# Sixteen indirect stores of a routing list, held one by one for the exponentials of the next batch's causal attention

## The reference

```python
att = jnp.einsum('bhqd,bhkd->bhqk', q, k) / jnp.sqrt(jnp.float32(hd))
att = jnp.where(causal, att, -jnp.inf)
att = jax.nn.softmax(att, axis=-1)
y = jnp.einsum('bhqk,bhkd->bhqd', att, v)
...
logits = flat @ gate_W + gate_b
top_v, top_i = jax.lax.top_k(logits, TOP_K)
w = jax.nn.softmax(top_v, axis=-1)
w_full = w_full.at[jnp.arange(N)[:, None], top_i].add(w)
for e in range(NUM_EXPERTS):
    mid = jax.nn.gelu(flat @ exp_W1[e] + exp_b1[e], approximate=False)
    out = out + w_full[:, e:e + 1] * (mid @ exp_W2[e] + exp_b2[e])
```

## Time and profile before

| | us |
|---|---|
| median of 3 runs (lowest, highest) | 4084.98 (4074.66, 4093.1) |
| the profiled execution | 4093.66 |
| its span, first to last instruction | 4091.9 |
| TensorE busy in it (matmuls) | 3443.6 |
| VectorE busy | 2301.5 |
| ScalarE busy | 1529.2 |
| GpSimd busy | 432.3 |

### The profile page before, as it was taken

The page is one execution under the profiler, slowest core; times in us unless marked ns, Lnnn a source line. Parts: engine busy times, 40 slices in busy tenths (PEclk is TensorE's granted clock), DMA queues, the critical chain, the costliest instruction groups (busy, mean ns, idle before and its releaser), DMA issues.

```text
span 4091.9 us, 55117 instructions
## 1 busy us (share of the span) xinstructions
PE 3443.6 (84%) x21294; PEld 1851.1 (45%) x21294; DVE 2301.5 (56%) x5198; ACT 1529.2 (37%) x2358; POOL 432.3 (11%) x323
## 2 busy tenths in 40 slices
PE   7788887787797589998889888898888988889988
PEld 5333333433432378886445324463244543344532
DVE  7664663673664356665643565634657246564356
ACT  5354343434334234443542323523234332254232
POOL 0000000001001134443000020000210001100002
PEclk9899898989989789999999998998998999999989
DMA  7401400410320497775111302113021032201130
GB/s 280 108 10 64 116 10 7 161 22 5 133 53 2 77 264 222 222 228 154 25 27 27 69 6 58 27 25 66 5 53 34 4 38 58 50 15 27 27 69 11
DMA packets 197242, 292.19 MB, mean 71 GB/s; under 512 B 88125, under 2 KB 154319, under 8 KB 180241
## 3 DMA queue, kind: packets, MB, share of 16 engines
q1 hardware_dynamic: 179957, 268.10, 24.8%
q0 software_dynamic: 17024, 20.53, 2.5%
HBM read 210.02 MB, written 77.23 MB: 70 GB/s over the span
## 4 chain that ended last, share of the span: by engine, by line
PE 55%; DVE 24%; ACT 8%; DMA 6%; issue 5%; SPq 1%; POOL 1%; another core or an unknown queue 0%; DVEq 0%; ACTq 0%; POOLq 0%
PE ps L877 6%; DVE max_parts L2097 5%; PE ps L827 5%; PE ps L829 4%; PE ps L828 4%; PE ps L1036 4%; PE ps L1265 3%; PE ps L1272 3%; PE ps L996 3%; PE ps L1158 2%; PE ps L1419 2%; PE ps L1019 2%; DMA q_stack<-in_exp_W 2%; PE ps L1193 2%; ACT arena L1538 2%
## 5 line engine op out<-in xcount | busy, mean ns | idle before, releaser
L877 PE MATMUL ps<-ternary_W,ident 128*128 128x512 f16 x2260 | 677.2, 415 | 134.4 <-ACT arena L1665 40.8
L2097 DVE TENSOR_REDUCE max_parts<-ps 128x1 f32<-128x512 f32 (+3 forms) x768 | 384.4, 551 | 196.4 <-PE ps L999 122.4
L1538 ACT ACTIVATE arena<-ps 128x256 f32<-128x256 f32 (+7 forms) x512 | 318.8, 650 | 447.3 <-PE ps L1019 258.0
L877 PEld LDWEIGHTS ps<-ternary_W,ident 128*128 128x128 f16 x2260 | 226.9, 105 | 454.4 <-issue 152.5
L1848 POOL TENSOR_TENSOR arena<-arena 128x640 f32<-128x640 f32 x96 | 154.9, 1614 | 1999.8 <-ACT arena L1770 1998.6
L2017 DVE CAST arena<-arena 128x256 f16<-128x256 f32 (+2 forms) x424 | 162.0, 382 | 255.0 <-ACT arena L1702 136.0
L1604 ACT ACTIVATE arena<-ps 77x1024 f32<-77x1024 f32 x192 | 190.6, 1017 | 196.7 <-PE ps L1185 194.0
L1770 ACT ACTIVATE arena<-ps 128x1024 f32<-128x1024 f32 x128 | 130.7, 1024 | 335.2 <-PE ps L1408 328.9
L996 PE MATMUL ps<-k_stack,q_stack 96*128 96x512 f16 (+3 forms) x576 | 196.6, 378 | 65.5 <-DVE max_parts L2097 32.8
L2019 DVE TENSOR_TENSOR arena<-arena 128x256 f16<-128x256 f32 (+2 forms) x424 | 241.6, 570 | 14.7
L2532 DVE TENSOR_REDUCE max_parts<-ps 128x1 f32<-128x512 f32 x256 | 166.5, 686 | 143.1 <-PE ps L1392 141.3
(11 more groups left out here) (444 smaller groups left out, 7395.4 us busy)
## 6 DMA issues: line engine op xcount, KB each, us to landing
arena<-scr_expert_weights SPq DMA_DIRECT2D x52, 1024.0 KB
k_stack<-scr_expert_weights SPq DMA_DIRECT2D x26, 1024.0 KB
q_stack<-in_exp_W SPq DMA_DIRECT2D x16, 1024.0 KB
scr_expert_weights<-k_stack SPq DMA_DIRECT2D x16, 1024.0 KB, 4.9
q_stack<-scr_q SPq DMA_DIRECT2D x108, 128.0 KB, 3.8
scr_q<-arena SPq DMA_DIRECT2D x48, 256.0 KB, 2.3
k_stack<-scr_q SPq DMA_DIRECT2D x72, 128.0 KB, 4.7
scr_q<-arena SPq DMA_DIRECT2D x16, 512.0 KB, 4.2
```

Source lines behind the costliest of these rows:

```text
L877: pe.matmul(s[:, 0:CH], ident[:], Wq1[:, 0, 0:CH], start=True, stop=True)
L1538: act.activation(PR[:, n % NP, kt * P:T], slot(L, "ST", g, kt, j)[:, kt * P:T], ACT.Exp).then_inc(*did("act", L, "exp", g, kt, j))
L2097: dve.tensor_reduce(mpart[:, j * NT + t, c:c + 1], slot(L, "S", g, t, j, c)[:, 0:n], AX, ALU.max).then_inc(*frees("dve", L, "S", g, t, j, c))
```

## The change

The first of a batch's sixteen stores goes out as before, when the list's entries are there. Each of the other fifteen first waits for one exponential of the next batch's attention: that of the last head (j = 3) of the tiles (2, 0), (2, 1) to (3, 6) in turn, the two last groups of heads. The stores themselves, their order and what they write are the same. For the last batch, which has no batch after it, nothing changes.

```diff
--- before.py
+++ after.py
@@ -1794,8 +1794,12 @@
             def note_places(b):
 
                 pool.wait_ge(*of("dve", "RT", "entry", batch=b))
+                among = [(g, kt) for g in range(2, NG) for kt in range(NT)] if b + 1 < NB else []
                 for t in range(NT):
                     for i in range(2):
+                        if among and t + i:
+                            g, kt = among[2 * t + i - 1]
+                            pool.wait_ge(*of("act", "B0", "exp", g, kt, GH - 1, batch=b + 1))
                         pool.indirect_dma_start(d_tab, bass.IndirectOffsetOnAxis(ap=slots_now[:, t, i:i + 1], axis=0),
                                                 entry[:, t, i], None).then_inc(*did("st_tab", b, t, i))
```

## The result

The changed kernel takes 4048.0 us, the median of five runs (4043.68 to 4052.79). The kernel before, timed again beside it, takes 4086.42 (five runs, 4074.66 to 4093.1). The ratio is 0.990, its 95% interval 0.9883 to 0.9916: 38.4 us saved, between 34 and 48 us by the interval. The forecast was 4043 with 42 us saved.

A forecast was written before the change was run, and what follows sets the result against it. It took sixteen crowded stores delaying TensorE's signals in three batches' attention as the loss on the path that sets the end. 42.85 us regained less 1 for moved stores, 42 rounded, off the 4084.98 median gave 4043 us; range 4030 to 4076.

The forecast's parts named there:

- The size of the loss: Attention from the tick (once-per-group reduction) of g = 2 to that of g = 3: batches 1 to 3 lose 42.85 us against batch 0.
- The cost of a spread store: Each of 45 moved stores was priced at 0.02 us, 1 us in all; bounds were zero and 0.89 us each.
- Stage A: Attention from the tick (once-per-group reduction) of g = 2 to that of g = 3; forecast at 43 to 46 us in all batches.
- Who is late: Beside the row of stores, TensorE's signals to ScalarE and VectorE come late, by 7.2 us, though their inputs are ready.
- something was still empty: Feared error: the row's first stores were free only because something was empty that a later isolated store finds full; no size.
- Crowding: The forecast's case: only a row of stores at 1.27 us delays TensorE's signals; 4043 us, chance 0.79.
- The ports rule: Skill page on SBUF ports: DMAs and compute cannot slow each other, so the saving would be zero instead of 42 us.
- not the stores: Rival: the attention loss stems from the routing itself, the stores only lie beside it; no change, 4085 us, chance 0.04.
- The sum: Whole kernel: 42.85 us regained less 1 us for the moved stores, rounded to 42 us gained.
- all later stages shift earlier with it: Stages after the shortened attention stage hang on signals, so the 42 us saved reaches the end.
- rival on the slower side: Each moved store in the attention catches a TensorE signal: 95 us lost against 43 gained, +52, 4137 us; chance 0.07.
- stage g = 3: From the tick of g = 3 to the end of the attention's exponentials; forecast 39 to 41 us, well over 45 if slower.

The follow-up runs named there:

- none: Changed kernel without the stores of the first three batches and VectorE's wait for them, so the list is incomplete; 4040.14 us.
- gap1: Changed kernel with its exponential waits replaced, in three batches, by a 128x416 GpSimd clearing between two stores, pitch 1.60 us; 4048.55 us.
- gap_small: Changed kernel with its exponential waits replaced, in three batches, by a 128x32 GpSimd clearing between two stores, pitch 1.28 us; 4098.79 us.
- row_in_g3: Changed kernel with all sixteen stores of each of three batches in one row after the first exponential tile of g = 3; 4088.9 us.
- Fours: Changed kernel with a store waiting for an exponential only every fourth time, giving rows of four at 1.27 us; 4045.35 us.
- narrow: Changed kernel without exponential waits, stores in one row at the old place, each of 16 partitions instead of 128 in three batches; 4094.31 us.
- landed: Changed kernel with each store waiting for the landing of the one before instead of an exponential, last batch included; 4088.91 us.
- last_too: Changed kernel with the last batch's stores also spread, each held for an eviction of the context keys by ScalarE; 4045.54 us.
- busy_pool: Changed kernel with forty 128x416 clearings on GpSimd ahead of the spread stores in the first three batches; 4056.69 us.

## Why the prediction was right

*The size of the loss.* The term was 42.85 us, from batches 1 to 3 against batch 0. Measured in the same stage of the two profiled executions: 175.33 - 132.82 = 42.51. A batch that lacks the suspected cause was a good ruler; it is the step to copy.

*The cost of a spread store.* Taken at 0.02 us, with 0.89 as the other bound. Stage A with the spread stores is not longer than without any (none), so 0 within the 1.3 us by which this stage varies from run to run. The first stores of the row were the right rows to price it by. The pitch of "about 5 us" is 4.8 on average in batch 1, with 1.88 us the closest, and the bound of the pair gap1 and gap_small lies below that.

*Who is late.* The prediction said TensorE's signals to ScalarE and VectorE. The trace settles this further than its views do, for it also records when each semaphore was counted up. In the changed kernel, over stage A of batch 1, TensorE's semaphore is counted up 0.01 to 0.05 us after the end of the matmul, with 94 such records for the 95 matmuls that count it up. In the kernel before, the count that lets the exponential start at 622.47 us is recorded at 622.45, and its matmul had ended at 615.24. So it is the count itself that comes late, and not a reader that is slow to see it. In the changed kernel the late starts are gone, and row_in_g3 brings them back at another place, 8.8 us late. It also feared that the first stores were free only because something was still empty. Fours and the changed kernel answer that: after a pause the next stores are free again.

*What was too coarse.* "Crowding" stood for a row as such. What counts is the rate: a row of sixteen at 1.60 us is free (gap1). The wait for exponentials is one way to a lower rate, and its places in the attention are of no account.

*The ports rule.* The rival "not the stores" is the one that the Trainium skill would have had by its page "SBUF — State Buffer", section "SBUF: two separate sides", where neither a DMA nor a compute instruction can slow the other. On durations the trace agrees: the stores take 0.97 us and ScalarE is busy 21.4 us in stage A, with the row or without; TensorE's matmuls take longer only with the lower granted clock. Starts are another thing: taking the stores away, or issuing them 0.3 us further apart, gives back 14 us a batch. The measurement decides.

*The sum.* The profiled executions differ by 40.9 us, 42 were predicted. Part of this closeness is luck: by the first pick of the expert phase the saving is 38.3 us, and the last 2.6 come after it, where nothing was changed. The 42.5 of stage A do not all arrive: by the ticks batch 1's g = 3 is 14.64 us earlier, batch 2's g = 2 only 12.16, batch 3's g = 2 22.59, its g = 3 36.40. So 2.5 and 3.5 us go missing between the batches, against "all later stages shift earlier with it". One such stretch in the changed kernel, then the same work in the kernel before:

```profile
762.13:785.72 23.59, 18.89 (x107) 10.10 (x105) 18.61 (x52) 5.08 (x9) 0.00 (x0) 0.93 0.00 1
```

```profile
776.25:798.99 22.74, 17.44 (x107) 9.75 (x105) 17.95 (x52) 5.08 (x8) 0.00 (x0) 1.00 0.00 1
```

The same 107 matmuls are busy 1.45 us longer at a granted clock of 0.93 than at 1.00. I don't put this down to the change. From batch 1's last copy to batch 2's first tick the kernel before took 146.9 us in this execution, the changed one 149.5, but narrow and gap_small, which keep the whole loss, took 151.3 and 149.9. It varies between executions, and the execution of before had it short; why is not shown.

*Against the medians* the saving is 38.4 us where 42 was forecast; the interval of 34 to 48 us holds 42, so no term is shown to be wrong by this. The rival on the slower side, a signal caught by each moved store, fell with the stage g = 3, for which it asked well over 45 us. The prediction measured that stage to an end 1.31 us behind the start of the last pair of copies (363.50 in the earlier trace rows against 362.19), and by that end the three batches take 39.3, 38.1 and 38.1 us where it said 39 to 41: at the lower edge and just under it, since a store costs nothing there either.

Two expectations behind the prediction failed for one reason: landed and last_too both misjudged the last batch. There the list is needed by the next phase, so its last landing counts, and the row's crowding counts little (2 to 5 us).

## What to carry to other kernels

Small DMAs issued back to back by GpSimd can hold up TensorE's signals to other engines while the DMAs and the readers' instructions take as long as ever: look for waits put down to "remote" beside such a row, and compare the stage with one that has no row. The remedy is a lower rate, and it costs nothing: a clearing of 0.45 us between two stores, or rows of four with pauses, did as well here as waits placed by hand. A chain of waits on landings also lowers the rate, but where the next phase needs the last store it gives the gain away again.

## What the runs showed of the hardware

- A store of one list column by indirect DMA takes GpSimd 0.97 us (0.85 with 16 partitions) and 0.30 us to the next one; chained by landings the pitch is 3.1 to 3.5 us in the first three batches. In the last there were single waits of 12.7 and 9.4 us while the DMA engines had other work: their share was 1.25 and 0.67 in those two stretches (a packet counts where it starts, so a share can pass 1) and 0.01 from then on.
- At a pitch of 1.15 to 1.28 us sixteen such stores delayed TensorE's signals by 7.2 us (kernel before), 8.8 us (row_in_g3) and 12.9 us (narrow) and cost a stage of the attention 13 to 16 us; at 1.60 us nothing. A row of four at 1.27 us is free, one of eight costs 5 us. At the end of phase 0 the same row of sixteen cost 2 to 5 us.
- What the stores and TensorE's signals share is open. The size of a store plays no part (narrow), nor does GpSimd's other work (busy_pool). The page "DMA: Bandwidth & Descriptors" of the Trainium skill, section "Why a DMA increments its semaphore by 16 and not by 1", says that a DMA issued by GpSimd counts up its semaphore by one from each of 16 engines whatever its shape. The traces agree for whole stores: in landed 1024 counts are recorded for its 64, 16 each. For stores of 16 partitions they can't tell, since in close rows most counts are missing from the record: 42 to 46 are there for sixteen such stores, 52 to 71 of 256 for the rows of the kernel before, 164 to 196 in gap1. If every store makes its 16, a row at 1.27 us makes 12.6 per us and one at 1.60 makes 10.0, an estimate from the two pitches. A limit on counts per time between the two, shared with TensorE's, would fit the pair of gap1 and gap_small; it would not tell why the last batch's row costs so little, and it remains a guess.
- Two rivals stay untested. Whether DMAs of another queue at the same rate do the same, no run shows. And every time here, also of the executions without a kept trace, comes with a recorded span and clock, so no run shows what the row costs in an execution of which nothing is recorded; that some counts go missing from the record in just these rows makes it worth asking.
